# A value product ahead of the scores: reordering one unit of a cross-attention kernel on three engines

## The reference

```python
q = split_heads(x @ Wq.T)                      # 20 heads of 32
k, v = split_heads(text @ Wk.T), split_heads(text @ Wv.T)
out_text = merge_heads(softmax(q k^T / sqrt(32)) v)
k_ip, v_ip = split_heads(ip @ Wk_ip.T), split_heads(ip @ Wv_ip.T)
out_ip = merge_heads(softmax(q k_ip^T / sqrt(32)) v_ip)
return (out_text + out_ip) @ Wo.T + bo + x
```

## Time and profile before

| | |
|---|---|
| median of 3 executions | 515.15 us (514.61 to 518.61) |
| the profiled execution | 518.32 us, its span 516.5 us |
| PE busy | 491.9 us (95%) |
| PEld busy | 417.1 us (81%) |
| DVE busy | 419.9 us (81%) |
| ACT busy | 369.9 us (72%) |
| POOL busy | 310.9 us (60%) |

### The profile page before, as it was taken

One profiled execution on the slowest core, in us unless ns is written; L12 is line 12 of the kernel. 1 busy time (PEld: TensorE's weight loads), 2 busy tenths in 40 slices (PEclk: granted clock), 3 DMA queues, 4 the chain that ended last, 5 costly groups with the idle time before them and its releaser, 6 DMA issues.

```text
span 516.5 us, 16128 instructions
## 1 busy us (share of the span) xinstructions
PE 491.9 (95%) x5314; PEld 417.1 (81%) x5314; DVE 419.9 (81%) x650; ACT 369.9 (72%) x1691; POOL 310.9 (60%) x320
## 2 busy tenths in 40 slices
PE   7699988799999999999999999999999999999787
PEld 7699986588888888888878888888878888788575
DVE  0307955989999999999999999999999999999822
ACT  0516775777887887878878878878777878778710
POOL 2205575456857667767667676667576677655530
PEclk9889999899999999999999999999999999999999
DMA  8968826999999999999999999999999999999994
GB/s 277 404 260 334 264 83 187 296 267 293 293 293 294 298 317 305 315 317 301 315 309 303 314 299 295 305 301 294 309 300 293 310 311 297 311 281 295 295 278 135
DMA packets 104574, 149.15 MB, mean 289 GB/s; under 512 B 11744, under 2 KB 91104, under 8 KB 104416
## 3 DMA queue, kind: packets, MB, share of 16 engines
q1 hardware_dynamic: 104544, 148.77, 95.8%
HBM read 85.81 MB, written 62.91 MB: 288 GB/s over the span
## 4 chain that ended last, share of the span: by engine, by line
POOL 39%; issue 37%; PE 12%; DMA 3%; ACT 3%; SPq 3%; POOLq 1%; DVE 1%; DVEq 0%
POOL probs L364 21%; POOL res L370 9%; POOL x_lo L355 9%; PE q_ps L702 3%; DMA stage<-wk_in 3%; PE s_ps L829 2%; PE pv_ps L829 2%; ACT probs L423 1%; PE v_ps L829 1%; PE s_ps L727 1%; POOLq L105 1%; SPq L302 1%; PE s_ps L778 1%; SPq L255 1%; DMA p_last<-bounce_d 1%
## 5 line engine op out<-in xcount | busy, mean ns | idle before, releaser
L364 POOL TENSOR_TENSOR probs<-probs,row_inv 128x616 f32<-128x616 f32 x160 | 193.6, 1231 | 163.8 <-DVE row_inv L621 163.8
L423 ACT ACTIVATE probs<-s_ps,row_neg 128x77 f32<-128x77 f32 x640 | 200.4, 339 | 73.5 <-DVE row_neg L589 73.5
L589 DVE TENSOR_REDUCE row_neg<-s_ps 128x8 f32<-128x616 f32 x160 | 120.4, 794 | 26.3 <-PE s_ps L727 23.2
L423 ACT ACTIVATION_READ_ACCUMULATOR probs<-s_ps,row_neg 128x1 f32 x640 | 140.9, 220 | 0.0
L609 DVE STREAM_TRANSPOSE turned<-probs 128x512 f32<-128x512 f32 (+1 forms) x160 | 125.0, 819 | 1.8 <-POOL probs L364 1.8
L702 PEld LDWEIGHTS q_ps<-x_hi,wq_hi 128*128 128x128 f32 x400 | 58.0, 189 | 32.1 <-issue 30.6
L702 PE MATMUL q_ps<-x_hi,wq_hi 128*128 128x256 f32 x400 | 81.7, 301 | 1.3 <-ACT q L413 1.3
L616 DVE TENSOR_REDUCE row_sum<-probs 128x8 f32<-128x616 f32 x80 | 63.6, 795 | 16.3 <-ACT probs L432 16.3
L702 PE MATMUL q_ps<-x_hi,wq_lo 128*128 128x256 f32 x400 | 72.9, 279 | 0.0
L702 PE MATMUL q_ps<-x_lo,wq_hi 128*128 128x256 f32 x400 | 72.8, 279 | 0.0
L727 PE MATMUL s_ps<-keys,q 32*128 32x154 f32 x1280 | 64.9, 317 | 3.5 <-ACT probs L423 1.8
(11 more groups left out here) (78 smaller groups left out, 623.4 us busy)
## 6 DMA issues: line engine op xcount, KB each, us to landing
bounce_d<-turned SPq DMA_DIRECT2D x80, 640.0 KB, 5.5
p_main<-bounce_d SPq DMA_DIRECT2D x320, 128.0 KB
res<-x_in SPq DMA_DIRECT2D x75, 128.0 KB, 4.9
y_out<-res SPq DMA_DIRECT2D x75, 128.0 KB, 4.6
x_raw<-x_in SPq DMA_DIRECT2D x70, 128.0 KB, 4.7
p_last<-bounce_d SPq DMA_DIRECT2D x80, 104.0 KB
stage<-wk_in SPq DMA_DIRECT2D x6, 640.0 KB, 10.7
stage<-wv_in SPq DMA_DIRECT2D x6, 640.0 KB, 10.5
```

The costliest lines, as they stand in the source:

```text
L364: nc.gpsimd.tensor_tensor(rows[:, :, keys], rows[:, :, keys], row_inv[:, u.slot, :, br].unsqueeze(2) .broadcast_to([P, GROUP * SUB, size]) ...
L423: done = nc.scalar.activation(rows[:, cols], s_ps[:, j, cols], ACT.Exp, bias=row_neg[:, j, i:i + 1], accum_out=row_sum[:, j, i:i + 1])
L589: nc.vector.tensor_reduce(row_neg[:, heads_of(half)], by_row(s_ps[:, heads_of(half), 0:SUB * BLK]), AXIS.X, ALU.max, negate=True).then_inc ...
```

## The change

In the fill and in `emit` alike three steps are moved within their unit; no instruction is added or removed. TensorE does `weigh_values(u-5)` ahead of `scores(u)`. ScalarE does `attn_high(u-5)` ahead of all exponentials of unit u, so that it follows `next_x(u-1)`. VectorE does `attn_low(u-5)` ahead of `find_max(u)`, so that it follows `invert(u-1)`. In the fill, ScalarE's calls for unit 7 are written out in that order, and TensorE does `weigh_values(2)` ahead of `scores(7)`.

```diff
--- before.py
+++ after.py
@@ -432,10 +432,9 @@
                 nc.scalar.activation(rows, rows, ACT.Exp).then_inc(exp_done, 1)
 
             def exps(u):
-                exp_direct(u, range(0, 1))
                 if u.plus(-VALUE_LAG).exists():
                     attn_high(u.plus(-VALUE_LAG))
-                exp_direct(u, range(1, PAIR))
+                exp_direct(u, range(PAIR))
                 exp(u)
 
             def split_x(u):
@@ -550,7 +549,9 @@
             keep_q(Unit(0, 7))
             keep_q(Unit(0, 8))
             next_x(Unit(0, 6))
-            exps(Unit(0, 7))
+            attn_high(Unit(0, 2))
+            exp_direct(Unit(0, 7), range(PAIR))
+            exp(Unit(0, 7))
             keep_q(Unit(0, 9))
             attn_high(Unit(0, 3))
             exp_direct(Unit(0, 8), range(PAIR))
@@ -635,14 +636,14 @@
                                                in1=last_place(c), op0=ALU.add, op1=ALU.add).then_inc(last_added, 1)
 
             def emit(u):
+                if u.plus(-VALUE_LAG).exists():
+                    attn_low(u.plus(-VALUE_LAG))
                 for half in range(2):
                     find_max(u, half)
                 take_max(u)
                 if u.plus(-1).exists():
                     for part in range(BRANCHES):
                         turn(u.plus(-1), part)
-                if u.plus(-VALUE_LAG).exists():
-                    attn_low(u.plus(-VALUE_LAG))
                 invert(u)
 
             def keep_v(br):
@@ -808,9 +809,9 @@
             def emit(u):
 
                 chunk = u.plus(-OUT_LAG)
-                scores(u)
                 if u.plus(-VALUE_LAG).exists():
                     weigh_values(u.plus(-VALUE_LAG))
+                scores(u)
                 if u.plus(Q_AHEAD).exists():
                     project_q(u.plus(Q_AHEAD))
                 if chunk.exists():
@@ -889,8 +890,8 @@
             weigh_values(units[1])
             project_q(units[7])
             project_q(units[8])
+            weigh_values(units[2])
             scores(units[7])
-            weigh_values(units[2])
             project_q(units[9])
             weigh_values(units[3])
             scores(units[8])
```

## The result

The changed kernel takes 521.20 us (median of 14, of which 13 lie between 519.4 and 524.9), the one before 515.22 beside it: a ratio of 1.0118 with a 95% interval of 1.0093 to 1.0143. The changed kernel is slower, as forecast, but by 6 us and not by 21.

A forecast was written before the change was run, and what follows sets the result against it. TensorE and the ring VectorE, ScalarE, VectorE were taken to bound the kernel together, transfers close behind. Profiled 518.32 + 17.8 (new ring) + 2.5 = 538.6 us, or 535.4 by the median; forecast 536.5, range 528 to 549.

The forecast's parts named there:

- a ring over ScalarE and VectorE: Loop: exponentials, rest of ScalarE's list, `attn_high`, `attn_low`, `find_max`, next exponentials; 5.49 us plus 0.30 per x copy, +17.8 us.
- `keep_q` to `add_bias` 0.52 when it isn't held: ScalarE's list in unit 38: step of 0.52 us (257.69 to 258.21), taken as unheld, in the 3.91 us of ScalarE's part.
- the round trip from `attn_high` to the first exponential: From ScalarE over VectorE's `attn_low` and `find_max` back to ScalarE: 1.58 us per unit, read from the fill.
- second way to the same sum: Stretch of 69 units: ScalarE's busy 308.1, gaps of 0.09 (6.2) and `attn_high` end to exponential (82.8) give 397.1 us.
- The middle between 538.6 and 535.4: Whole kernel: typical time if longer units of the profiled execution are covered (538.6) or not (535.4); rounded to 536.5 us.
- The other ring: Through VectorE's own list, now with `attn_low`: 5.55 us, deciding only in units without an x copy, some 1 us in all.
- The drain and fill: Fill 0 (bounds -1.4 and +1.2); last interval and loop turns +1 to +2; with VectorE's ring +2.5 us.
- The correction of +3.2 for the longer profiled execution: Whole kernel: profiled execution is 3.2 us above the median; typical time after is 538.6 if covered by the longer ring, else 535.4.
- The hops cost more in the loop: Rival: `attn_high` to `attn_low` and `attn_low` to `find_max` each 0.15 dearer, about 557 us, with one 547; chance 0.18.
- The x copies don't count: Rival: slack in ScalarE's list swallows the 18.9 us of x copies; no change, 514 to 517 us; chance 0.06.
- Faster: Rival: `invert` still runs when `attn_high` ends, so the wait is free and exponentials lose 0.27 us; 511.5 or 508; chance 0.04.
- costs TensorE nothing in itself: TensorE, `weigh_values` ahead of `scores`: both products take 1.74 us before, 1.73 in the new order; taken as 0, upper end +4.

## Why the prediction was wrong

**What held.** The mechanism of the forecast is what the runs show: `attn_low` ahead of `find_max` closes a ring over ScalarE and VectorE, ScalarE's idle time becomes a link of it, and each x copy adds 0.30. The slope came out as forecast (5.29, 5.58, 5.89; and 5.30, 5.90, 6.51 with the copies doubled). So did ScalarE's waits for the maxima (82.4 us, forecast 83). The level did not come out: 5.5, 5.8 and 6.1 were forecast.

**What failed is one term of the sum.** The prediction took "`keep_q` to `add_bias` 0.52 when it isn't held (257.69 to 258.21)". It was held. TensorE's row of the kernel before that belongs to it:

```profile
257.90 0.28 PE L702 MATMUL x_ps<-attn_lo,wo_hi 128*128 128x256 f32 x1
```

It ends at 258.18, and `add_bias` starts at 258.21. The row of `add_bias` names no wait, since the gap behind `keep_q` is only 0.09 long, and I read the lack of a bracket as freedom. `keep_q` is itself 0.43 long, and the engine would start the next copy before its end. In the changed kernel, where the output product is long done, the step is 0.27 (259.03 to 259.30), and 0.26 or 0.27 in every unit of the loop. The kernel before with fewer matmuls shows the same without any move, as was forecast for it. There the last matmul of the output product ends at 121.66, well ahead, and the step is 0.27:

```profile
121.38 0.28 PE L702 MATMUL x_ps<-attn_lo,wo_hi 128*128 128x256 f32 x1
...
122.37 0.43 ACT L413 ACTIVATE q<-q_ps 128x256 f32<-128x256 f32 x1
122.64 0.53 ACT L457 ACTIVATE y<-x_ps,bo 128x256 f32<-128x256 f32 x1
```

That is 0.25 less in 69 units, 17.3 us. The other term that moved is the round trip from `attn_high` to the first exponential, 1.63 to 1.65 instead of 1.58, 69 x 0.05 = 3.5 us. The sum corrected: 397.7 - 17.3 + 3.5 = 383.9, and a turn of the loop costs some 0.12 five times, 384.5. Measured: 384.2.

The "second way to the same sum" was not independent of the first. It took its 0.09 of gap from the same two rows, and ScalarE's busy time with the full length of rows that overlap once nothing holds them.

Two smaller slips changed nothing in the outcome. The middle between 538.6 and 535.4 is 537.0 and not 536.5. And the two engines of the ring were not at "81% each" in the stretch: ScalarE was (308.12 of 380), VectorE was at 93% (354.76).

**The other ring**, through VectorE's list, was put at 5.55, from a step of 0.33 between reciprocal and `find_max`. That step, too, was a wait for the scores without a bracket. VectorE's timeline after:

```profile
260.04 0.25 DVE L622 RECIPROCAL row_inv<-row_sum 128x16 f32<-128x16 f32 x1
260.20 0.36 DVE L626 TENSOR_TENSOR attn_lo<-pv_ps,attn_hi 128x256 fp32r<-128x256 f32 x1
260.48 1.50 DVE L590 TENSOR_REDUCE row_neg<-s_ps 128x8 f32<-128x616 f32 x2
...
265.33 0.25 DVE L622 RECIPROCAL row_inv<-row_sum 128x16 f32<-128x16 f32 x1
266.02 0.42 DVE L626 TENSOR_TENSOR attn_lo<-pv_ps,attn_hi 128x256 fp32r<-128x256 f32 x1 [0.44 <-ACT attn_hi L461]
266.36 1.50 DVE L590 TENSOR_REDUCE row_neg<-s_ps 128x8 f32<-128x616 f32 x2
```

Where VectorE isn't held (260.04) the step is 0.16, and `find_max` follows `attn_low` after 0.28. That ring is 5.29 long, the interval of a unit without a copy. The waits view has `attn_low`'s wait in only 17 units, those with two copies and the turns of the loop: 6.6 us, where I had said 20 and "in most units". In units with one copy the wait is there without a bracket: the step from the reciprocal to `attn_low` is 0.38 or 0.39 in them, and 0.16 to 0.18 in units without a copy.

By the sentence that I weighed (the Trainium skill, "VectorE: DVE Perf Modes", The DRAIN you can't avoid) `find_max` would have started no sooner than the 0.36 of `attn_low`; the trace has 0.28. The same section goes on that a next operation that isn't held starts earlier, which the prediction left out.

**What bounds the kernel before.** The prediction named TensorE and VectorE's ring together. VectorE's ring had slack, which is now seen in its step of 0.16 and in the 5.25 that the kernel with fewer matmuls reaches. The prediction's "VectorE never waited for the scores" was wrong. TensorE alternates between 5.41 and 5.47, and so does everything else where nothing disturbs it. The changed kernel takes 5.57 on average, against some 5.44 in undisturbed units before (5.51 over all 69 of the profiled execution), and not 5.76.

**The drain and fill** were put at +2.5, with the turns of the loop; they came out as -0.9 in the fill, +0.05 in the interval of unit 78 to 79 and -0.2 behind it. The correction of +3.2 for the longer profiled execution was half right: a ring as long as the new one covers the longer units between 357 and 413 us, so the gap of the medians is larger than that of the two spans.

**The rivals.** "The hops cost more in the loop" is refuted but for its 0.05. "The x copies don't count" is refuted by the doubled copies. "Faster" rested on `invert` still running when `attn_high` ends; in units without a copy it is so (5.29, below TensorE's 5.44), as the prediction said, and in the others not. The range's lower end of 528 had no bound for a step that was shorter than its row. That is the error behind the error: I bounded the terms that I didn't know, and left out those that I thought I had read. And the statement that TensorE's order "costs TensorE nothing in itself" is true only beside the move of `attn_low`; alone it costs 9%, since the value product then waits for `attn_low` of the unit before.

The Trainium skill ("Perfetto Trace Analysis", Identifying the Most-Contended Engine) says that matmul busy time is no good measure of how close TensorE is to its limit. The runs agree: TensorE's row is 99% busy after (376.01 of 380) and a tenth of its work could be taken away without gaining anything. The same section's rule, that the engine with the highest occupancy is the one to improve, is of little help here. That would be VectorE (349.55 of 380), but in units with x copies what sets the pace is ScalarE's list, at 297.55, together with the part of VectorE's that it waits for.

## What to carry to other kernels

A step from one instruction's start to the next is free only if the producer had finished well before; look up the producer's end in its own engine's timeline before a step goes into a sum that is multiplied by the number of units, since a short hold shows no wait. Moving an instruction that waits for another engine ahead of what that engine waits for turns idle time into a link, and everything in the queue ahead of its partner, optional copies too, then costs its full step. Of a reorder on several engines each part is to be followed around all its rings with the others left out: here each half alone costs 9%, and the whole 1.2%.

## What the runs showed of the hardware

An activation of 256 columns that is 0.41 to 0.52 us long in its row takes 0.26 to 0.35 us of ScalarE's time from start to start when the next one isn't held (`keep_q` 0.27, `add_bias` 0.35, x copy 0.31, one more x copy in each unit 0.30). The rows get longer when they overlap: `add_bias` is 0.47 in the kernel before and 0.51 in the changed one, where nothing holds it. On VectorE the reciprocal takes 0.16 to 0.18 from start to start with a row of 0.25, and `attn_low` 0.28 with a row of 0.36.
